# A decoder layer on one core: the expert FFN computed for the chosen tokens only, in 39 static tiles of 128 rows

## The chip, the cores and the metric

The kernel runs on one core of a Trainium2 chip. The metric is the device time of one execution in microseconds. Each comparison is between medians of several runs. The profile is one further execution, and its own time stands beside its span below.

## What is computed

The layer has three parts, each followed by a residual addition and a normalisation without learned scale. The input x has 2048 tokens of width 256.

```
x = norm(x + causal self attention with rotary turns, 16 heads of 16)
x = norm(x + cross attention over one context row per query:
        scores = (x Wq) ctx^T ; idx = argmax ; mem = ctx[idx]
        k, v = mem Wkv ; 16 heads share k and v ; softmax over the 2048 picked rows)
x = norm(x + ffn(x))

ffn: probs = sigmoid(x router^T)            # 8 experts
     topw, sel = top_k(probs, 2); topw /= sum
     h = relu(x W1_e)^2                     # width 256 for experts 0-3, 512 for 4-7
     out = sum over the two chosen experts of topw * (h W2_e)
```

All experts together are 3072 hidden columns wide, which is 24 tiles of 128. Each token needs two experts only.

## The kernel before

The program is a row of blocks. Inside a block each engine has its own list of instructions in a fixed order, and waits on semaphores. Between two blocks all engines meet.

The blocks are the projections with rotary turns, the causal self attention, projection and norm, the choice of a context row for each query, and then one last block with all the rest. The change touches only the last block, apart from small renamings and moved tiles. The last block is entered after a flag is read into a register (`either`). This flag picks the variant for at most 512 distinct context rows.

The last block before the change does two things at once:

- Cross attention in 16 units, for 4 chunks `c` of 512 tokens times 4 groups of heads. A unit has 16 "pieces": TensorE computes 128x512 scores (line 1467) and VectorE reduces each to a row maximum (line 1649). The maxima are turned (1470), negated and written back as extra rows of the operand through a DMA. Then come four steps. In each, TensorE makes four score tiles (1528), ScalarE takes their exponential in two instructions (1617), and TensorE multiplies them with the values (1537). The "sums" item divides (1665, 1671). The pieces of a unit are laid out ahead of the unit's steps by `just_in_time`.
- Everything behind a chunk, as side items laid out by `merge` between the thirds of the attention's steps. There are norm items (turn back 1479, projection 1486, statistics 1686, root 1442 on GpSimd, norm 1696, turn 1492, router logits, gates 1706 to 1725). There are 24 "hid" items per chunk: six matmuls of 512 columns in split fp32r (two parts of each operand, three products, two halves of the contraction, helper `product`, line 95), then relu, square, square on ScalarE (1595, 1599, 1600) and the remainder on VectorE (1729). There are 32 "y" items per chunk, 6 or 12 matmuls of 256 columns each. For each y item VectorE multiplies with the gate and adds to x (1738). Every token goes through every expert, and the gate is zero for six of eight.

Side items share three PSUM banks in turn (`SB`). `merge` gives them out by a budget of columns (`PACE`), so that the FFN of chunk c lies beside the attention of chunk c+1. After the last attention unit the FFN of chunk 3 runs alone. GpSimd splits the weights into two parts early in this block (1431, 1433). It issues no DMA anywhere, all of them go through the SP queue.

## Time and profile before

| | |
|---|---|
| median of 3 runs | 1313.38 us (1313.14 to 1318.69) |
| profiled execution, its own time | 1319.66 us |
| its span, first to last instruction | 1318.0 us |
| PE busy | 1172.4 us (89%) |
| DVE busy | 905.0 us (69%) |
| ACT busy | 674.1 us (51%) |
| POOL busy | 175.6 us (13%) |
| mean granted TensorE clock | 0.934 |

PE is TensorE, PEld its weight loads, DVE VectorE, ACT ScalarE, POOL GpSimd and SP SyncE, which only issues DMAs here. A matmul's busy time contains its latency and overlaps the next one. So the distance between the starts of two matmuls tells more than the length of one.

### The profile page before, as it was taken

The page shows a single profiled execution, that of the slowest core. Times are in us where ns is not written, and L with a number is a line of the kernel's source. Part 1 is how long each engine was busy: PE and PEld are TensorE (multiplying, and loading weights), DVE is VectorE, ACT ScalarE, POOL GpSimd, SP SyncE. Part 2 cuts the span into 40 slices and gives each one's busy share as a digit, 9 for nine tenths or more (in the row PEclk, how much of TensorE's full clock was granted, in tenths as well). Part 3 has the DMA queues.
Part 4 walks back from the last instruction along what each step waited for, and adds up shares of the span by engine and source line. Part 5 has one row for each costly group of instructions (what it writes and reads, how often), then busy time and mean ns, then how long its engine had stood idle before and what let it go on. Part 6 is the DMA issues. An engine that isn't in the chain of part 4 may idle for free. (4 is left out here: it accounts for less than half of the span.)

```text
span 1318.0 us, 18684 instructions
## 1 busy us (share of the span) xinstructions
PE 1172.4 (89%) x6943; PEld 636.2 (48%) x6943; DVE 905.0 (69%) x1799; ACT 674.1 (51%) x951; POOL 175.6 (13%) x167
## 2 busy tenths in 40 slices
PE   6854999999999999974799699899989999999896
PEld 3531233333333333243688423456655665567785
DVE  3564999898888888127499799575657666634543
ACT  1320256666766666842343136456654665575463
POOL 2223111021021100033100265000000000000000
PEclk9885799999999999987799779899989999999999
DMA  6214167920000000030200053000000000000000
GB/s 237 93 49 106 25 75 79 110 28 1 2 1 1 1 1 2 1 134 0 75 26 24 28 163 96 13 13 13 13 13 29 13 13 13 17 1 1 17 1 19
DMA packets 45049, 51.03 MB, mean 39 GB/s; under 512 B 8122, under 2 KB 40506, under 8 KB 44954
## 3 DMA queue, kind: packets, MB, share of 16 engines
q1 hardware_dynamic: 44954, 49.78, 16.6%
q8 instruction: 58, 0.95, 0.3%
q14 instruction: 37, 0.30, 0.1%
HBM read 37.64 MB, written 11.53 MB: 37 GB/s over the span
## 5 line engine op out<-in xcount | busy, mean ns | idle before, releaser
L628 DVE TENSOR_REDUCE self_piece_max<-self_max 128x1 f32<-128x512 f32 (+3 forms) x640 | 349.3, 604 | 52.0 <-PE self_max L530 25.4
L595 ACT ACTIVATE self_probs<-self_scores 128x1024 f32<-128x1024 f32 (+3 forms) x320 | 274.1, 896 | 192.5 <-PE self_scores L549 191.6
L1649 DVE TENSOR_REDUCE cross_piece_max<-banks 128x1 f32<-128x512 f32 x256 | 167.0, 684 | 83.3 <-PE banks L1467 82.8
L530 PE MATMUL self_max<-stack_k,stack_q 96*128 96x512 bf16 (+3 forms) x640 | 209.2, 365 | 12.5 <-DMA stack_k<-kparts 6.4
L1617 ACT ACTIVATE cross_probs<-banks 128x1024 f32<-128x1024 f32 x128 | 128.7, 1018 | 110.0 <-PE banks L1528 109.1
L549 PE MATMUL self_scores<-stack_q,stack_k 98*128 98x512 bf16 (+3 forms) x640 | 170.3, 350 | 4.3 <-DMA stack_q<-self_shift 3.0
L560 PE MATMUL self_out<-self_probs,V 128*17 128x512 f32 (+3 forms) x1280 | 148.3, 535 | 2.6 <-ACT self_probs L595 2.0
L530 PEld LDWEIGHTS self_max<-stack_k,stack_q 96*128 96x128 bf16 x640 | 62.0, 98 | 181.0 <-DVE self_piece_max L628 130.8
L95 PE MATMUL banks<-w_first,hid_first 128*128 128x256 f32 x384 | 118.6, 309 | 7.7 <-DVE hid_rest L1729 4.2
L1595 ACT ACTIVATE o_tok<-banks 128x512 f32<-128x512 f32 x96 | 56.9, 592 | 112.3 <-PE banks L95 111.2
L1729 DVE TENSOR_TENSOR hid_rest<-o_tok,hid_first 128x512 fp32r<-128x512 f32 x96 | 65.5, 687 | 62.1 <-ACT o_tok L1600 61.9
L95 PE MATMUL banks<-w_rest,hid_first 128*128 128x256 f32 x384 | 107.7, 280 | 0.0
L95 PE MATMUL banks<-w_first,hid_rest 128*128 128x256 f32 x384 | 107.6, 280 | 0.0
L1467 PE MATMUL banks<-kx_few,stackx 97*128 97x512 bf16 x256 | 94.0, 408 | 8.4 <-DVE cross_piece_max L1649 4.0
L95 PE MATMUL banks<-x2T_first,w_first 128*128 128x512 f32 x192 | 85.9, 447 | 9.0 <-DVE x2T_rest L1701 7.3
L497 POOL TENSOR_SCALAR_AFFINE_SELECT self_probs<-self_probs 128x512 f32<-128x512 f32 x64 | 40.8, 637 | 397.2 <-ACT self_probs L595 396.9
L1738 DVE SCALAR_TENSOR_TENSOR x_sb<-banks,mix,x_sb 128x256 f32<-128x256 f32 x128 | 60.0, 480 | 41.9 <-PE banks L95 40.7
L95 PEld LDWEIGHTS banks<-w_first,hid_first 128*128 128x128 f32 x384 | 72.8, 190 | 24.1 <-DVE x_sb L1738 9.1
L549 PEld LDWEIGHTS self_scores<-stack_q,stack_k 98*128 98x128 bf16 x640 | 57.0, 98 | 54.0 <-ACT self_probs L595 16.3
L1528 PE MATMUL banks<-stackx,kx_few 99*128 99x512 bf16 x256 | 79.5, 393 | 0.5 <-DMA stackx<-cross_shift 0.5
L95 PE MATMUL banks<-x2T_first,w_rest 128*128 128x512 f32 x192 | 77.4, 403 | 0.0
L95 PE MATMUL banks<-x2T_rest,w_first 128*128 128x512 f32 x192 | 77.3, 402 | 0.0
(219 smaller groups left out, 1704.3 us busy)
## 6 DMA issues: line engine op xcount, KB each, us to landing
stack_q<-qparts SPq DMA_DIRECT2D x96, 64.0 KB, 8.2
stackx<-xparts SPq DMA_DIRECT2D x96, 64.0 KB, 2.3
o_tok<-in_w SPq DMA_DIRECT2D x8, 768.0 KB, 5.6
stack_k<-kparts SPq DMA_DIRECT2D x18, 256.0 KB, 13.1
qparts<-parts SPq DMA_DIRECT2D x8, 384.0 KB, 2.5
kparts<-parts SPq DMA_DIRECT2D x8, 384.0 KB, 2.5
xparts<-xparts_sb SPq DMA_DIRECT2D x8, 384.0 KB, 2.8
xT_sb<-in_xT SPq DMA_DIRECT2D x4, 512.0 KB, 8.1
```

Of the source, the lines that this page charges most:

```text
L95: ins = nc.tensor.matmul(out, lhsT[a], rhs[b], start=first and n == 0, stop=last and n == len(terms) - 1)
L530: mm = nc.tensor.matmul(slot[:, 0:pc["w"]], pc["lhsT"], pc["rhs"], start=True, stop=not pc["diag"])
L549: mm = nc.tensor.matmul(ps[:, j, st["off"]:C], st["keys"](j), st["queries"](j), start=True, stop=True)
L560: mm = nc.tensor.matmul(po[32 * j:32 * j + VW, st["off"]:C], st["values"](j), probs[:, i % 3, j, st["off"]:C], start=st["first"], stop=st[ ...
L595: nc.scalar.activation(probs[:, i % 3, 2 * pair:2 * pair + 2, st["off"]:C], ps[:, 2 * pair:2 * pair + 2, st["off"]:C], ACT.Exp, scale=SCAL ...
L628: nc.vector.tensor_reduce(piece_max[:, u % 2, pc["row"], pc["at"]:pc["at"] + 1], slot[:, 0:pc["w"]], AX.X, ALU.max).then_inc(side_read, 1)
L1467: mm = nc.tensor.matmul(slot[:, 0:pc["w"]], pc["lhsT"], pc["rhs"], start=True, stop=True)
L1528: mm = nc.tensor.matmul(ps[:, j], st["keys"](j), st["queries"](j), start=True, stop=True)
L1617: nc.scalar.activation(probs[:, i % 3, 2 * pair:2 * pair + 2], ps[:, 2 * pair:2 * pair + 2], ACT.Exp, scale=SCALE).then_inc(probs_ready, 1)
L1649: nc.vector.tensor_reduce(piece_max[:, u % 2, pc["row"], pc["at"]:pc["at"] + 1], slot[:, 0:pc["w"]], AX.X, ALU.max).then_inc(side_read, 1)
L1729: nc.vector.tensor_tensor(hid[1][:, h % HR], relu[:, h % 2], hid[0][:, h % HR].bitcast(F32), ALU.subtract).then_inc(hid_ready, 1)
L1738: nc.vector.scalar_tensor_tensor(out=x_sb[:, n], in0=slot[:, 0:D], scalar=mix[:, c % 2, q, e:e + 1], in1=x_sb[:, n], op0=ALU.mult, op1=ALU ...
```

## The change

The last block is split into two.

The first block keeps the cross attention and the norm items. `merge` is replaced by `weave`, a list of items per chunk with fixed distances in thirds of a step. Behind the gates there are new items. "copy" (ScalarE, two copies of the chunk's rows into `xd`). "gate" (VectorE; it writes the weight and the number of the return row beside each row). "rank" (14 tiny matmuls count the tokens before each one in its expert's list, then eight VectorE instructions). "send" (GpSimd, eight indirect DMAs of 128 rows of 258 floats into the expert regions `sent` in device memory). After chunk 3 comes "table", some 20 VectorE instructions on one partition, which make the tables of the 39 tiles: source row, offset in W1, offset in W2. SP then reads eight row numbers into registers and writes eight blocks of padding rows. The weights of W2 are kept four tiles wide for each expert, and VectorE zeroes the unused ones at the block's start.

The second block runs 39 tiles of 128 rows. Of each tile the SP queue loads 128 rows from `sent`, at a row number read into a register, into one of four buffers (`XR`). A buffer is free when the tile that used it has been written back. TensorE turns the rows, computes 512 hidden columns, turns these back, and multiplies with W2. The weight offsets are read into registers on TensorE, twice for each tile. GpSimd writes the 128 result rows with an indirect DMA to `ybuf`. When all 39 tiles are written, both result rows of every token are loaded again, added to x, and x is normalised and stored.

```diff
+TILES = (2 * T + E * (P - 1)) // P          # 39
+ROW = D + 2
+XR = 4
-                def merge(steps, works, first_of, before, thirds):
+                def weave(steps, works, first_of, before, thirds):
+                    todo = [item for c in range(NC) for item in (
+                        ("back", c, 0, 1), ("back", c, 1, 0), ("proj", c, 0, 2), ("proj", c, 1, 0), ("stats", c, 0, 1), ("norm", c, 0, 5),
+                        ("x2t", c, 0, 1), ("x2t", c, 1, 0), ("logit", c, 0, 2), ("ltr", c, 0, 2), ("copy", c, 0, 0), ("gate", c, 0, 1),
+                        ("rank", c, 0, 4), ("send", c, 0, 1))]
...
+                                elif item[0] == "send":
+                                    for q in range(TC):
+                                        for k in range(2):
+                                            nc.gpsimd.indirect_dma_start(
+                                                sent[:], bass.IndirectOffsetOnAxis(place[:, k, q], 0), xd[:, k, q], None).then_inc(s_sent, 16)
+                            pool.wait_ge(probs_used, len(steps))
+                            nc.gpsimd.memset(pads[:, :, 0:D + 1], 0.0).then_inc(pads_ready, 1)
...
+                        sp.wait_ge(pads_ready, 2)
+                        sp.dma_start(sent[E * CAP:].rearrange("(b p) d -> p b d", p=P), pads[:, E:]).then_inc(s_pad, 16)
+                        sp.wait_ge(tab_ready, 1)
+                        for e in range(E):
+                            row = sp.value_load(pad_at[0:1, e:e + 1], min_val=0, max_val=E * CAP - P)
+                            sp.dma_start(sent[bass.ds(row, P)], pads[:, e]).then_inc(s_pad, 16)
...
+                    # SP, second block
+                    for i in range(TILES):
+                        if i >= XR:
+                            sp.wait_ge(s_y[i % XR], 16 * (i // XR))
+                        row = sp.value_load(tab[0:1, 0, i:i + 1], ...)
+                        sp.dma_start(xin[:, i % XR], sent[bass.ds(row, P)]).then_inc(s_xin[i % XR], 16)
+                    # GpSimd
+                    for i in range(TILES):
+                        pool.wait_ge(y_read, i + 1)
+                        nc.gpsimd.indirect_dma_start(ybuf[:], bass.IndirectOffsetOnAxis(xin[:, i % XR, D + 1:ROW].bitcast(U32), 0),
+                                                     ys[:, i % XR], None).then_inc(s_y[i % XR], 16)
+                    # TensorE
+                    for i in range(TILES):
+                        if i + 1 < TILES:
+                            hidden(i + 1)         # value_load, 6 matmuls of 512 columns
+                        if i + 2 < TILES:
+                            turn_in(i + 2)        # waits s_xin, 2 transposes
+                        output(i)                 # value_load, 12 matmuls of 256 columns
+                        if i + 1 < TILES:
+                            turn_back(i + 1)      # 4 transposes
+                    # ScalarE: relu, copy of the turned rows, two squares for each tile
+                    # VectorE: remainder of the rows, scaling of the output, remainder of the squares
+                    # after tile 38: eight loads of 512 KB, two additions (GpSimd, VectorE), statistics, root, norm, 16 stores
```

## Rows read from the trace of the kernel before

**Rows 1.** Windows of the last block: stretch, its length, busy time of each engine, clock, DMA
```profile
751.00:769.60 18.60, 14.14 (x31) 4.08 (x32) 13.03 (x25) 1.28 (x1) 14.36 (x11) 0.50 0.44 142
...
788.30:825.50 37.20, 36.53 (x209) 11.41 (x207) 34.18 (x65) 25.38 (x28) 19.54 (x8) 1.00 0.31 97
...
860.00:1198.00 338.00, 323.20 (x1889) 204.73 (x1888) 209.62 (x468) 197.58 (x292) 4.04 (x4) 0.98 0.05 14
1198.00:1318.00 120.00, 102.83 (x659) 90.33 (x658) 57.59 (x146) 55.50 (x101) 3.02 (x3) 0.98 0.03 10
```

**Rows 2.** Groups from 750.5 us on: busy, mean ns | idle before, releasers
```profile
L1649 DVE TENSOR_REDUCE cross_piece_max<-banks 128x1 f32<-128x512 f32 x256 | 167.0, 684 | 83.3 <-PE banks L1467 82.8
L1617 ACT ACTIVATE cross_probs<-banks 128x1024 f32<-128x1024 f32 x128 | 128.7, 1018 | 110.0 <-PE banks L1528 109.1
L95 PE MATMUL banks<-w_first,hid_first 128*128 128x256 f32 x384 | 118.6, 309 | 7.7 <-DVE hid_rest L1729 4.2 <-DVE x_sb L1738 2.8 <-DVE cross_piece_max L1649 0.4
...
L95 PE MATMUL banks<-x2T_first,w_first 128*128 128x512 f32 x192 | 85.9, 447 | 9.0 <-DVE x2T_rest L1701 7.3 <-DVE x_sb L1738 0.8 <-ACT o_tok L1595 0.2
...
L1729 DVE TENSOR_TENSOR hid_rest<-o_tok,hid_first 128x512 fp32r<-128x512 f32 x96 | 65.5, 687 | 62.1 <-ACT o_tok L1600 61.9
...
L1433 POOL TENSOR_TENSOR w_rest<-o_tok,w_first 128x1536 fp32r<-128x1536 f32 x8 | 27.5, 3442 | 0.6
...
L1607 ACT COPY cross_acc<-banks 128x512 f32<-128x512 f32 x16 | 9.3, 579 | 6.4 <-PE banks L1537 6.4
```

**Rows 3.** Chain that ended last: start, us, what
```profile
1228.80 4.42 PE banks L95 x18
...
1292.19 7.26 PE banks L95 x54
```

**Rows 4.** Writers of banks, 769 to 826 us: durations, first and last start
```profile
L1665 DVE RECIPROCAL cross_inverse<-banks x4: 246/248/248, 788.3 to 825.5; 128x16 f32<-128x16 f32 x4
```

**Rows 5.** Timeline of DVE, 828 to 845 us: start, us, what, idle before
```profile
828.74 0.69 DVE L1649 TENSOR_REDUCE cross_piece_max<-banks 128x1 f32<-128x512 f32 x1 [1.96 <-PE banks L1467]
...
831.51 0.69 DVE L1677 TENSOR_TENSOR x_sb<-banks,x_sb 128x512 f32<-128x512 f32 x1 [0.64 <-PE banks L1486]
833.24 0.69 DVE L1677 TENSOR_TENSOR x_sb<-banks,x_sb 128x512 f32<-128x512 f32 x1 [1.03 <-PE banks L1486]
...
844.00 1.29 DVE L1701 TENSOR_TENSOR x2T_rest<-banks,x2T_first 128x512 fp32r<-128x512 f32 x2 [0.83 <-ACT x2T_first L1581]
```

**Rows 6.** Timeline of chunk 3 behind its attention
```profile
1198.99 1.04 PE L1479 MATMUL banks<-ident,o_tok 128*128 128x128 f32 x8
...
1202.15 3.69 PE L1486 MATMUL banks<-xwc_sb,o_tok 128*128 128x256 f32 x16 [0.63 <-ACT o_tok L1577]
...
1207.69 1.40 DVE L1686 BATCH_NORM_STATS2 norm_stats<-x_sb 128x6 f32<-128x256 f32 x4
...
1209.85 1.01 POOL L1442 TENSOR_TENSOR norm_rstd<-norm_rstd,minus_half 128x4 f32<-128x4 f32 x1 [68.70 <-DVE norm_rstd L1691]
```

**Rows 7.** Timeline of the gates of chunk 0, first and last of 22 instructions
```profile
859.00 0.17 DVE L1706 TENSOR_SCALAR gate<-gate 128x32 f32<-128x32 f32 x1
...
861.91 0.19 DVE L1723 TENSOR_TENSOR hot<-hot,top 128x32 f32<-128x32 f32 x1
```

**Rows 8.** Timeline at the entry of the last block
```profile
749.88 0.59 ACT L1046 CAST kx_few<-pp 99x512 bf16<-99x512 f32 x1 [2.06 <-PE pp L1008]
...
751.47 1.28 ACT L1617 ACT_TABLE_LOAD   x1 [1.01 <-PEq L910]
```

**Rows 9.** DMA issues: what, count, KB each, median us from issue to landing
```profile
stackx<-xparts SPq DMA_DIRECT2D x96, 64.0 KB, 2.3
...
out<-x_sb SPq DMA_DIRECT2D x16, 128.0 KB, 1.8
...
x_sb<-in_x SPq DMA_DIRECT2D x1, 1536.0 KB, 8.8
```

**Rows 10.** SP's issues of the tile stackx: ns min/median/max, first and last start
```profile
L1376 SPq DMA_DIRECT2D stackx<-xparts x96: 303/426/1888, 750.9 to 1094.3; - x96
```

More of the change, by code:

```diff
@@ L44 @@
 SX = 4
-HR = 6
-PACE = 0.9
 LOW = -3.0e38
@@ L139, in decoder_layer @@
         tri_b = sb(top, "tri_b", [P, P], BF16)
+        ones_b = sb(top, "ones_b", [P, P], BF16)
+        below_b = sb(top, "below_b", [P, P], BF16)
         consts_in = sem("consts_in")
@@ L515, in program @@
                             loaded, reads, freed = [0], [0], []
-                            nc.tensor.matmul(po[:], zeros[:, 0:P], zeros[:], start=True, stop=True)
+                            for n in range(C // P):
+                                nc.tensor.matmul(po[:, n * P:(n + 1) * P], zeros[:], zeros[:], start=True, stop=True)
                             def side_item(item):
@@ L1197, in plan @@
-            def plan(keys, vals, n):
-                steps, works = [], []
-                width = C if n == FEW else n // 4
-                for c in range(NC):
-                    for g in range(NG):
-                        u = c * NG + g
-                        here = stackx[:, u % SX]
-                        pieces = [dict(w=width, lhsT=here[0:KS + 1, j, q * P:(q + 1) * P],
-                                       rhs=keys[0:KS + 1, a * width:(a + 1) * width], row=j * GH + q, at=a)
-                                  for j in range(GH) for q in range(C // P) for a in range(n // width)]
-                        works.append(dict(pieces=pieces, shift_to=[
-                            here[KS + 1 + b:KS + 2 + b].rearrange("o h (n t) -> o (h n) t", t=P) for b in range(2)]))
-                        for t in range(n // P):
-                            steps.append(dict(unit=u, diag=0, first=t == 0, last=t == n // P - 1,
-                                              keys=lambda j, t=t: keys[0:KS + 3, t * P:(t + 1) * P],
-                                              queries=lambda j, u=u: stackx[0:KS + 3, u % SX, j, :],
-                                              values=lambda j, t=t: vals(t)))
-                return steps, works
@@ L1217, in columns @@
-            def columns(item):
-                kind = item[0]
-                if kind in ("hid", "logit"):
-                    return 3 * KD * C
-                if kind == "y":
-                    return 3 * (WIDTHS[item[2]] // P) * D
-                if kind == "proj":
-                    return 4 * 2 * KD * D
-                return 4 * C if kind in ("back", "x2t") else 0
-            def just_in_time(steps, works):
-                per, length = len(works[0]["pieces"]), len(steps) // len(works)
-                maxima = [("piece", u, k) for u in range(len(works)) for k in range(per)]
-                given = per + per // 3
-                before = maxima[0:per] + [("turn", 0)] + maxima[per:given]
-                thirds = [[[], [], []] for _ in range(len(steps) + 3)]
-                late = []
-                for i in range(len(steps)):
-                    want = min(len(maxima), per + -(-per * (i + 3) // length))
-                    new = maxima[given:want]
-                    given = max(given, want)
-                    for k in range(3):
-                        late = [(n - 1, item) for n, item in late]
-                        thirds[i][k] += [item for n, item in late if n == 0]
-                        late = [(n, item) for n, item in late if n]
-                        mine = new[(k * len(new) + 2) // 3:((k + 1) * len(new) + 2) // 3]
-                        thirds[i][k] += mine
-                        late += [(2, ("turn", item[1])) for item in mine if item[2] == per - 1]
-                assert not late and given == len(maxima)
-                for i, step in enumerate(steps):
-                    if step["last"]:
-                        thirds[i + 2][0].append(("sums", step["unit"]))
-                return steps, works, {u: u * length for u in range(len(works))}, before, thirds
@@ L1355, in decoder_layer @@
[L1355 to L1368 removed]
+            stage = ExitStack()
@@ new lines, in decoder_layer @@
+            xin = sb(tail, "xin", [P, XR, ROW])
+            xT = [sb(tail, f"xT_{n}", [P, 2, KD, P], F32R) for n in ("first", "rest")]
+            act_of = sb(tail, "act_of", [P, 2, C])
+            hT = [sb(tail, f"hT_{n}", [P, 2, 4, P], F32R) for n in ("first", "rest")]
+            square = sb(tail, "square", [P, 2, C])
+            ys = sb(tail, "ys", [P, XR, D])
+            yb = sb(tail, "yb", [P, 2, NT, D])
+            px = psum(tail, "px", [P, 2, C])
+            ph = psum(tail, "ph", [P, 2, C])
@@ L1434, in _ @@
-                    pool.wait_ge(w_split, len(pieces_w) + 1)
-                    def program(steps, works, first_of, before, slots, at, read_at, copied_at, norm_at, stat_at):
-                        order = [it for step in slots for slot in step for it in slot if it[0] in ("stats", "fstats")]
-                        for k, (_, c) in enumerate(order):
-                            mine = rstd[:, TC * c:TC * (c + 1)]
-                            pool.wait_ge(s_ones2, SX + 1)
-                            pool.wait_ge(var_ready, k + 1)
-                            nc.gpsimd.tensor_tensor(mine, mine, minus_half[:], ALU.pow).then_inc(rstd_ready, 1)
@@ L1628, in _ @@
+                    turned_in(1)
+                    positive(0)
+                    squares(0)
+                    for i in range(TILES):
+                        if i + 1 < TILES:
+                            positive(i + 1)
+                        if i + 2 < TILES:
+                            turned_in(i + 2)
+                        if i + 1 < TILES:
+                            squares(i + 1)
                 @block.vector
                 def _(dve):
-                    chained = Count(sem("cross_dve_chain"))
@@ new lines, in _ @@
+                    turned_in(0)
+                    turned_in(1)
+                    rests(0)
+                    for i in range(TILES):
+                        if i + 2 < TILES:
+                            turned_in(i + 2)
+                        dve.wait_ge(y_ready, i + 1)
+                        if i >= XR:
+                            dve.wait_ge(s_y[i % XR], 16 * (i // XR))
+                        nc.vector.tensor_scalar(ys[:, i % XR], py[:, i % 2, 0:D], xin[:, i % XR, D:D + 1], None, ALU.mult).then_inc(y_read, 1)
+                        if i + 1 < TILES:
+                            rests(i + 1)
```

1171 lines of the change are left out of this document (668 added, 503 removed).

## The prediction

> **What bounds the kernel now.** I read the windows of the last block first [rows 1], since the change leaves the 751 us ahead of it alone. The block is 567 us long. In its first attention chunk, which has no FFN beside it, DVE is busy 34.2 of 37.2 us: attention alone is bound by the row maxima. From 860 us on PE is busy 323 of 338 us and DVE only 210: with the FFN beside it TensorE is the limit. The last 120 us are the FFN of chunk 3 by itself. Next the groups [rows 2]: the FFN is 576 matmuls of 512 columns (three groups of 192) and 1152 of 256 columns (three of 384). Their busy times overlap, so I take the distance between starts from the chain [rows 3]: 4.42 us for 18 matmuls of 512 columns is 0.245 us each, 7.26 us for 54 of 256 is 0.134 us. The FFN so costs 576 x 0.245 + 1152 x 0.134 = 141 + 154 = 295 us of TensorE. It falls to 234 x 0.245 + 468 x 0.134 = 57 + 63 = 120 us, plus turns. So 175 us leave TensorE. But they leave a block in which they lay beside DVE-bound attention, and what comes back is serial.
>
> **First block, attention with routing (from 751 us).** The attention of chunk 0 stays as it is. Its divisions are at 788.3 and 825.5 us, three units apart [rows 4]: 12.4 us for a unit of four steps, 3.1 us a step. The same pace holds for the following units, as there is no FFN to slow them, and DVE is what they wait for. From step 17 (825.5) to step 58, the last with pieces, are 41 steps: 127 us, to 952. To this come DVE's new and kept items for chunks 0 to 2, which sit on the binding engine and so count in full. For each chunk these are the projection's two additions 1.4; statistics 2.0 (1.4 for four [rows 6], aggregates 0.6); norm 1.4; two remainders 1.3 [rows 5]; gates 4.2 (22 instructions took 3.1 us from 859.0 to 862.1 [rows 7], now they are 25 with more of them waiting for the one before); rank about ten instructions of this size, 2.0. Sum 12.3. In that order DVE also waits: 1.96, 0.64, 1.03 and 0.83 us for PE and ACT in chunk 0 [rows 5], 4.5 us, and I take 5, between nothing and 8. So 3 x 17.3 = 52 us, to 1004. The remaining seven steps have no maxima and go at ACT's pace, 2 x 1.02 us [rows 2], with a last copy, turn and division: 15 us. The attention ends at 1019 us. In the kernel before, that point was 1198. ACT has room (25.4 of 37.2 us in three units [rows 1]). TensorE's records fill 36.5 of the 37.2 us, but they overlap, and by starts it has some too. GpSimd splits two more weight pieces, each two thirds of (1.5 + 3.4) us, in time for the first turn back by my estimate. Zeroing W2 on DVE (eight instructions of 128x512, 0.35 to 0.69 us each) lies in the 5 us in which DVE waits for the first operand; without this cover it is 5 us.
>
> **Behind chunk 3, all serial.** Turn back 1.0 and ACT 0.6, projection 3.7 (PE, 16 matmuls [rows 6]), addition 0.7, statistics 2.0, root 1.0, norm 1.4, turn, copy and remainder 2.5, logits 2.1, gate turn 0.7, gates 4.2, rank 1.2 on PE and 2.0 on DVE: with about 0.1 us for each handover 24 us, to 1043. Then GpSimd issues eight scatters of 128 rows. The trace has no indirect DMA. The nearest row below is SP's issue, 0.43 us [rows 10], the nearest above GpSimd's longest instruction, 3.44 us [rows 2]. I take 1.5 us, nearer to the issue since this is no elementwise work. So 12 us. GpSimd's list has the memset of the padding (3855 elements a partition, at its 1 us for a thousand, 4 us) behind them, and SP waits for it: 1059. The table on DVE (20 instructions, 6 us) is covered by this. SP issues one store, then eight times a register load and an issue. The entry of the old block bounds a register load with barrier, compare and branch at 1.0 us (750.47 to 751.47 [rows 8]) and so the load alone between 0 and 1; I take 0.5. Nine issues and eight loads are 8 us, landing 2, meeting of the engines 1: the second block starts at 1070 us (1061 to 1086).
>
> The Trainium skill (DMA: Bandwidth & Descriptors, Latency and other measured facts) puts the floor of a register load from memory at about 600 ns. By it the eight loads would be 0.8 us longer and the sum 0.8 us later.
>
> **The tiles.** Two loops compete.
> (a) TensorE in its own order: 6 x 0.245 + 12 x 0.134 + 6 turns x 0.13 (eight in 1.04 us [rows 6]) = 1.47 + 1.61 + 0.78 = 3.86 us. Two register loads come on top, each between 0 (queued matmuls cover it) and 1.0 us; I take 0.3, which makes 4.5. ACT has 0.37 + 3 x 0.58 = 2.1 us and DVE 0.4 + 0.4 + 0.69 = 1.5 us for a tile [rows 2]; both have room.
> (b) The return of a buffer. The turn of tile i+2 waits for the write-back of tile i-2. From the end of output(i-2): DVE's scaling 0.4, scatter issue 1.5, landing of 128 KB in device memory 1.8 [rows 9], SP's register load and issue 0.9, landing of the load 2.0 (between 1.8 and 2.3 [rows 9]), five handovers 0.5: 7.1 us. TensorE needs two periods less output(i-1) and one turn (1.9 us) to get there, so 2 P - 1.9 >= 7.1, P >= 4.5. With the scatter at 0.43 us P is 3.95, at 3.44 us it is 5.45.
> Both come to 4.5, and two loops of the same length on in-order engines lose a little: P = 4.7 us. The first tile needs 8.5 us from the start to the end of its output, 38 periods are 178.6, the last write-back 4.3: 191.4, to 1261.5 us.
>
> **The end.** Eight loads of 512 KB: 2 MB in all for the first two chunks, 4 MB by 18.6 us, at the rate of the 1.5 MB load behind the 0.5 MB one (2 MB in 9.3 us [rows 9]). Then for chunks 2 and 3, which no transfer covers any more: GpSimd's addition of 1024 elements 2.3 (3.44 for 1536), DVE's addition 1.3 and statistics 2.1, twice, norm 1.4 three times, handovers, last store 1.8: 15.9 us. Together 34.5, to 1296 us of span. The old end had 8 us from its last output to the last instruction.
>
> **Sum.** 751 + 268 + 51 + 191.4 + 34.5 = 1296 us of span against 1318.0, 22 us less. The profiled execution took 1319.66 us, 1.66 around its span, so its like is 1297.6. The median of the runs is 6.3 us below the profiled one; taken from the median, 1313.4 - 22 = 1291 us. Of the 175 us that leave TensorE 22 remain, since routing, padding, the fill of the tiles and the return are now behind one another.
>
> **Rivals.**
> (1) Cheaper DMAs: the scatter costs as little as SP's issue. P falls to about 4.0, bound by TensorE's 3.86 with register loads hidden: 38 x 0.7 = 27 us less, and 8 x 1.07 = 9 us less behind chunk 3. Time 1291 - 36 = 1255. For it: matmuls queue far ahead in this trace, with hardly a gap in L95's groups [rows 2]. Against: GpSimd computes each of 128 addresses, SP does not.
> (2) Slower than before: the scatter itself is dear, up to 3.44 us on GpSimd. It is paid 8 times behind chunk 3 (+15.5 us) and stands in loop (b), P = 5.45 (+28.5 us): 1335 us. Each further microsecond of scatter costs 8 + 19 = 27 us, so this decides from 2.3 us on, where the 22 us are gone. For it: small GpSimd work is slow here, four elements a partition take 1.01 us [rows 6]. Against: nothing but the guess of its kind.
> (3) The clock. In the stretch at the block's entry, where TensorE waited 0.5 us between single matmuls, 0.50 of full speed was granted (the 1.2 GHz level), and 1.00 (2.4 GHz) where it was dense [rows 1]. In the tile loop it works 3.9 of 4.7 us. If a sixth of the time went at the lower level, loop (a) is 5.1 us: +15 us, 1306.
> (4) GpSimd and DVE in each other's way. Rows first: GpSimd's eight subtractions took 3.44 us on the mean beside DVE's reductions from PSUM [rows 2], and no row shows what an instruction of DVE with SBUF operands does to them. In the tiles DVE's remainder of the squares has two operands in SBUF, 0.69 us. If it holds back the scatter each time, loop (b) is 0.69 longer, P + 0.35, +13 us: 1304. The Trainium skill (SBUF — State Buffer, the "DVE blocks DMA" trap) says that DVE instructions holding the shared port keep GpSimd from writing its descriptors; that rule speaks for this rival, and no row of this trace shows an indirect DMA.
>
> **Chances.** Forecast 0.40, (1) 0.17, (2) 0.25, (3) 0.08, (4) 0.10. The forecast's own range is 1274 to 1310. Measurements of this kernel tell about 0.5% (6.6 us) from no change: faster is below 1306.8, slower above 1320. Of the forecast 0.36 lies below that and 0.04 within; (1) is all faster, (3) and (4) fall half below and half within, (2) is slower but for 0.02. With a margin for unlisted stalls, which only lengthen: faster 0.56, same 0.15, slower 0.29. The range is 1250 to 1348: from a little under (1) to a little over (2).
>
> **What would show it.** The attention's last division near 1019 us with 12.4 us units; if later, routing stalls DVE or TensorE more than 5 us a chunk. GpSimd's scatter at 1.5 us; the second block's first load at 1070. Starts of the tiles' outputs 4.7 us apart, and TensorE's longest wait in a tile: if it is for the landed rows, loop (b) holds; if for nothing or for registers, loop (a). The last 35 us without matmuls. The prediction is wrong if the scatter takes over 2.3 us, if the tiles' period leaves 4.0 to 5.4, or if the serial piece behind chunk 3 is longer than 65 us.

## The result, and the profile of the changed kernel

The changed kernel takes 1309.2 us in the median of 12 runs (1301.62 to 1312.03); the kernel before took 1316.42 (12 runs, 1311.28 to 1321.62) beside it. The ratio is 0.9933, interval [0.9908, 0.9958]: about 7 us less, where 22 were forecast. The profiled execution took 1306.89 us, with a span of 1305.1 and a granted clock of 0.898. The same kernel run later (e10, two runs), on the chip that had e5 to e9, took 1300.76 and 1295.11 us, ratio 0.9869 [0.9833, 0.9905] to the kernel before beside it.

The page of the changed kernel: busy times, then groups (busy, mean ns, idle before), then DMA issues.

```profile
PE 1054.4 (81%) x6214; PEld 522.4 (40%) x6214; DVE 876.0 (67%) x1759; ACT 599.2 (46%) x827; POOL 261.0 (20%) x249
...
L1619 DVE TENSOR_REDUCE cross_piece_max<-banks 128x1 f32<-128x512 f32 x256 | 164.0, 683 | 30.4 <-PE banks L1441 25.5
...
L1786 POOL DMA_INDIRECT ybuf<-ys,xin x39 | 37.5, 960 | 160.4 <-DVE ys L1916 160.4
...
L1409 POOL DMA_INDIRECT sent<-xd,expert_place x32 | 31.3, 979 | 100.1 <-DVE chosen_b L1707 87.1
...
xin<-sent SPq DMA_DIRECT2D x39, 129.0 KB, 2.1
```

DVE's idle time before a row maximum fell from 83.3 to 30.4 us [rows 2]: the attention now goes at DVE's pace, as forecast. The scatter, which no row of before showed, takes 0.96 us of GpSimd. The windows show which limit replaces TensorE (columns as in [rows 1]): the serial piece behind the attention, then the tiles.

```profile
1028.40:1083.77 55.37, 10.48 (x57) 6.91 (x57) 16.20 (x71) 4.89 (x8) 12.47 (x11) 0.64 0.17 57
1100.00:1260.00 160.00, 136.61 (x836) 114.73 (x835) 55.55 (x104) 69.78 (x140) 33.59 (x35) 0.97 0.19 59
```

For 55 us no engine is busy a third of the time. In the tiles TensorE records 137 of 160 us, and this view of the waits between 1100 and 1268 us (total us, times, longest us) says what it waits for:

```profile
POOL ybuf L1786 <- DVE ys L1916: 134.3, 38, 6.0
...
PEld px L1812 <- DMA xin<-sent: 22.9, 18, 3.1
PE px L1812 <- DMA xin<-sent: 15.2, 17, 2.6
PEld py L1840 <- issue: 13.8, 21, 1.0
```

The same stretch as the chain of waits tells it, one turn of a buffer (start, us, what):

```profile
1095.90 0.50 DVE ys L1916
1096.39 0.27 issue
1096.66 2.40 DMA ybuf<-ys,xin
1099.07 0.27 SPq L1769
1099.37 0.15 SPq L1769
...
1099.79 2.11 DMA xin<-sent
1101.95 0.44 PE px L1812 x2
1102.38 0.41 issue
1102.80 1.24 PE py L1840 x8
1104.03 0.50 PE py L1843 x4
1104.55 0.50 DVE ys L1916
```

From a tile's scaling at 1095.90 to the turn of the tile that takes its buffer at 1101.95 are 6.05 us, and to the scaling of the tile two further on 8.65 us. That is two periods: loop (b), as forecast. At first the outputs follow each other at 3.48 and 5.1 us in turn. Later the distances lie between 3.5 and 5.4 us, with four longer ones (6.0, 6.2, 7.4, 6.9) and the last two at 3.3 and 3.1; the mean is 4.49. A wait for rows stands in about every second tile (18 for 38). The 0.41 us of "issue" behind the turn is the place of a register load. TensorE's first product of the output starts 0.85 us after the turn here, and 0.84 us in e2, where the turn takes 0.69 rather than 0.44 us. That the load sets this distance is argued, no run leaves it out.

The span in the prediction's terms, for the two profiled executions of the changed kernel ("again" is the later one) and the combined version further down. The first division is the first L1635 RECIPROCAL, the last its 16th; the second block starts with the first xin load; an output is a tile's L1916.

| term, us | forecast | changed | again | combined |
|---|---|---|---|---|
| start to first division | 788.3 | 792.4 | 791.5 | 786.5 |
| first to last division | 230.7 | 236.0 | 230.7 | 229.9 |
| last division to second block | 51 | 55.3 | 55.5 | 43.2 |
| second block to first output | 8.5 | 12.1 | 14.2 | 13.7 |
| 38 periods | 178.6 | 170.8 | 168.6 | 132.1 |
| last output to the end | 38.8 | 38.4 | 38.5 | 34.7 |
| span | 1296 | 1305.1 | 1299.0 | 1240.0 |

### The profile page after: what moved, and what is told of

Same layout as the page of the kernel before. It is cut to its first block and busy times, and to the rows that moved or that the text cites. A ratio compares the mean times of both kernels' runs of the same rounds, so it can differ in the third digit from the quotient of the medians.

```text
span 1305.1 us, 17932 instructions
## 1 busy us (share of the span) xinstructions
PE 1054.4 (81%) x6214; PEld 522.4 (40%) x6214; DVE 876.0 (67%) x1759; ACT 599.2 (46%) x827; POOL 261.0 (20%) x249
## 5 line engine op out<-in xcount | busy, mean ns | idle before, releaser
L538 PE MATMUL self_max<-stack_k,stack_q 96*128 96x512 bf16 (+3 forms) x640 | 209.4, 365 | 12.6 <-DMA stack_k<-kparts 6.4
L1619 DVE TENSOR_REDUCE cross_piece_max<-banks 128x1 f32<-128x512 f32 x256 | 164.0, 683 | 30.4 <-PE banks L1441 25.5
L1441 PE MATMUL banks<-kx_few,stackx 97*128 97x512 bf16 x256 | 95.3, 412 | 21.3 <-DVE cross_piece_max L1619 12.3
L1513 PE MATMUL banks<-cross_probs,vx_few 128*17 128x512 f32 x512 | 71.8, 635 | 0.4 <-ACT cross_probs L1583 0.4
L1441 PEld LDWEIGHTS banks<-kx_few,stackx 97*128 97x128 bf16 x256 | 25.4, 100 | 112.6 <-DVE cross_piece_max L1619 61.2
L1786 POOL DMA_INDIRECT ybuf<-ys,xin x39 | 37.5, 960 | 160.4 <-DVE ys L1916 160.4
L1899 DVE TENSOR_TENSOR xT_rest<-px,xT_first 128x256 fp32r<-128x256 f32 x39 | 16.6, 425 | 62.9 <-ACT xT_first L1865 62.8
L540 PE MATMUL self_max<-tri_b,ident_b 128*128 128x128 bf16 x256 | 58.5, 231 | 0.0
L1904 DVE TENSOR_TENSOR hT_rest<-square,hT_first 128x512 fp32r<-128x512 f32 x39 | 27.0, 692 | 46.9 <-ACT square L1879 46.9
L1878 ACT ACTIVATE hT_first<-pt 128x512 fp32r<-128x512 f32 x39 | 23.3, 598 | 70.0 <-PE pt L1829 70.0
L1812 PE MATMUL px<-ident,xin 128*128 128x128 f32 x78 | 16.2, 293 | 47.9 <-DMA xin<-sent 47.9
L1409 POOL DMA_INDIRECT sent<-xd,expert_place x32 | 31.3, 979 | 100.1 <-DVE chosen_b L1707 87.1
L98 PE MATMUL pp<-ctx_first,qp_first 128*128 128x512 f32 (+1 forms) x128 | 46.7, 365 | 3.2 <-DVE qp_rest L1065 2.0
```

The lines of the kernel that those rows point to most:

```text
L98: ins = nc.tensor.matmul(out, lhsT[a], rhs[b], start=first and n == 0, stop=last and n == len(terms) - 1)
L538: mm = nc.tensor.matmul(slot[:, 0:pc["w"]], pc["lhsT"], pc["rhs"], start=True, stop=not pc["diag"])
L540: mm = nc.tensor.matmul(slot[:, pc["w"] - P:pc["w"]], ident_b[:], tri_b[:], start=False, stop=True)
L1441: mm = nc.tensor.matmul(slot[:, 0:pc["w"]], pc["lhsT"], pc["rhs"], start=True, stop=True)
L1513: mm = nc.tensor.matmul(po[32 * j:32 * j + VW], st["values"](j), probs[:, i % 3, j], start=st["first"], stop=st["last"], tile_position=(0, ...
L1619: nc.vector.tensor_reduce(piece_max[:, u % 2, pc["row"], pc["at"]:pc["at"] + 1], slot[:, 0:pc["w"]], AX.X, ALU.max).then_inc(side_read, 1)
```

## Experiments

The theory behind them was this: the tiles go at the return of their buffers; zeroing and the serial piece take what is missing; the chunks' work costs more than its instructions since TensorE's turns and projections are spaced wrongly. The rivals are told in the expectations. All except the fourth edit the changed kernel; e10 is that kernel without an edit.

**e1: a ring of eight buffers.**

```diff
-XR = 4
+XR = 8
```

(The semaphores of the eight loads are ones that the block before has done with; that part of the edit is not shown.)

> Eight row buffers and result buffers instead of four (XR = 8), nothing else. Theory (the return of a buffer sets the period): with four buffers two tiles share one return of about 9 us, so outputs come 3.5 and 5.2 us apart, 4.49 on the mean. With eight, the return has six periods and binds no more; TensorE's own order is left, which the short periods of the changed kernel show as 3.5 us. 38 x (4.49 - 3.55) = 36 us less: tiles' outputs 3.5 to 3.6 us apart, time about 1273 us. Rival (register loads and TensorE's issue set the period, the waits for landed rows are only where that slack shows): period stays between 4.3 and 4.5, time within 5 us of the changed kernel, 1304 to 1314.

Measured: 1273.11 us (1272.01 to 1277.37), ratio 0.967 [0.9654, 0.9687]. Outputs are 3.49 us apart, and no wait for xin is left; the window, the waits of the tiles, and the outputs' line:

```profile
1120.00:1220.00 100.00, 100.00 (x691) 91.00 (x690) 46.01 (x87) 55.45 (x115) 26.92 (x28) 1.00 0.24 75
```

```profile
POOL ybuf L1787 <- DVE ys L1917: 91.0, 36, 2.9
ACT hT_first L1879 <- PE pt L1830: 44.4, 36, 1.3
```

```profile
L1917 DVE TENSOR_SCALAR ys<-py,xin x39: 482/484/486, 1104.1 to 1236.2; 128x256 f32<-128x256 f32 x39
```

38 periods last 132.1 us rather than 170.8. TensorE's own order is 3.48 us a tile. The forecast had 3.86 for its work alone, so the matmuls are a little cheaper than taken, and the 0.6 us for register loads in loop (a) do not show where matmuls are queued. This execution's attention was the longest of all (last division 1034.2), so 39 us in the tiles show as 30 in its span.

**e2: a ring of three**, `XR = 3`.

> Three buffers instead of four. Theory (return of a buffer): the turn of tile i+2 now waits for the write-back of tile i-1, one period less 1.7 us of TensorE after its output. The return itself takes 7.1 us (two mean periods of 4.49 less 1.9), so the period is 7.1 + 1.7 = 8.8 us, 38 x 4.3 = 164 us more: about 1470 us. Rival (TensorE's own order): the return has slack today, so the period is at most 5.5 us and the time at most 1350.

Measured: 1492.57 us, a single execution. The period is 9.75 us for most tiles (38 last 358.6 us), and TensorE waits for the rows in every tile (waits, then the window):

```profile
PEld px L1812 <- DMA xin<-sent: 118.3, 30, 4.6
```

```profile
1120.00:1440.00 320.00, 196.25 (x790) 162.25 (x789) 52.42 (x99) 67.47 (x131) 31.73 (x33) 0.74 0.09 28
```

With three buffers one period is a whole return and TensorE's part behind it. In one turn of the chain the return from scaling to turn takes 5.97 us (1151.56 to 1157.53), much as with four buffers. TensorE's part behind it takes 3.81 us rather than 2.60. The mean granted clock is 0.74 of full speed, so part of the stretch is at the lower level; TensorE is busy 196 of its 320 us. At 2.60 the period would be 8.6 us, at 3.81 it is 9.8. The expectation had 8.8 with a longer return and no loss of clock; it came out 23 us short, 0.6 us a tile. So rival (3) is real, but only with waits longer than those that four buffers leave: with four the clock is 0.97. Both experiments say the same: what four buffers cost is the return.

**e3: zeroing W2 on ScalarE** rather than on DVE.

```diff
...
-                                nc.vector.tensor_copy(w[:, e, 2:4].rearrange("p t (a d) -> p (t a) d", d=P),
-                                                      zeros[:].rearrange("p (a d) -> p a d", a=1).to_broadcast([P, 4, P]))
+                                nc.scalar.copy(w[:, e, 2:4].rearrange("p t (a d) -> p (t a) d", d=P),
+                                               zeros[:].rearrange("p (a d) -> p a d", a=1).to_broadcast([P, 4, P]))
...
```

> The eight instructions that zero the unused part of W2 run on ScalarE instead of VectorE; nothing else. Theory (VectorE's four copies of 2.09 us were held by GpSimd's memsets of the operand's ones rows, which run in the same 8 us): VectorE is free when the first scores are there, the first row maximum ends 4 to 5 us earlier, and all that follows is DVE-bound, so the time falls by 4 to 5 us: 1304 to 1305. Rival (the late start comes from the loads of the first operand, or ACT's copies now delay the first exponentials): within 1.5 us of the changed kernel.

Measured: 1300.58 us (1297.76 to 1306.91), ratio 0.9892 [0.987, 0.9914]. The timelines of the changed kernel and of this one at the block's entry:

```profile
749.78 8.12 DVE L1603 CAST w_first<-zeros 128x512 fp32r<-128x512 f32 x4 [1.94 <-PEq L916]
757.83 1.45 DVE L1603 CAST w_rest<-zeros 128x512 fp32r<-128x512 f32 x4
...
760.14 2.49 DVE L1619 TENSOR_REDUCE cross_piece_max<-banks 128x1 f32<-128x512 f32 x4 [0.73 <-DVE cross_piece_max L1605]
...
749.74 7.88 POOL L1380 MEMSET stackx<- 1x2048 bf16 x4 [115.43 <-POOLq L916]
```

```profile
750.38 2.17 ACT L1542 CAST w_first<-zeros 128x512 fp32r<-128x512 f32 x4 [0.45 <-PEq L916]
...
750.36 7.37 POOL L1380 MEMSET stackx<- 1x2048 bf16 x4 [116.40 <-POOLq L916]
...
755.55 4.87 DVE L1620 TENSOR_REDUCE cross_piece_max<-banks 128x1 f32<-128x512 f32 x8 [4.93 <-PE banks L1441]
```

Four casts of DVE take 8.12 us beside GpSimd's memsets, one cast to a memset, and the next four take 1.45: 2.03 us each against 0.36. On ScalarE the same casts beside the same memsets take 0.54 us each. The first row maximum begins 4.6 us sooner, and DVE waits 4.93 us for its operand: the cover was there, but the zeroing was twice its length. That the memsets make the casts slow is read from the two timelines, where each of the four casts begins up to 0.15 us behind a memset and ends 0.28 us behind it; no run leaves the memsets out. The rest of the median's 8.6 us is not shown to be this edit's. In the profiled execution it lies in the tiles, whose 38 periods took 166.1 us rather than 170.8, and this term moves without an edit too (168.6 us in e10).

The Trainium skill (SBUF — State Buffer, Who interferes with whom) says of the port pair that DVE and GpSimd share that, against a DVE instruction in a mode with two ports, whoever issues first holds it for the whole instruction. The durations agree, with 2.03 us for 0.36 us of work; the profile does not show the ports. The prediction weighed this only for the scatters in the tiles.

**e4: the dense kernel of before without its FFN.**

```diff
-                hidden = list(tiles)
+                hidden = []
-                values = [(c, e, q) for c in range(NC) for e in range(E) for q in range(TC)]
+                values = []
```

> The kernel before without its FFN: the hid, rest and y items are left out (the output is the normalised attention part alone); router, gates and both norms stay. Theory (attention and routing are bound by VectorE at 12.4 us a unit and 17 us of chunk work, so the dense FFN filled only TensorE's slack and cost nearly its whole length): the last division comes near 1018 us, the chain behind it about 30 us, end at 1050 us; the dense FFN so costs 265 of its 295 us, and the sparse one, 255 us with routing, fill, return and padding, is only 10 us shorter. Rival (the interleaving hides a good half of the dense FFN): the time is 1150 us or more.

Measured: 1056.45 us (two runs), ratio 0.8026 [0.8006, 0.8046]. The output of this kernel is the normalised attention part alone. Its divisions lie between 787.8 and 1024.1 us (1018 expected). That is 236.3 us, against 236.0 in the changed kernel, which starts them 4.6 us later. DVE and TensorE between them:

```profile
830.00:1010.00 180.00, 154.98 (x817) 54.23 (x815) 149.02 (x373) 94.04 (x107) 6.07 (x6) 0.93 0.10 30
```

The dense FFN costs 1316.4 - 1056.5 = 260 us of the time, for 295 us of TensorE: only 35 lay in the attention's shadow. The sparse one with its routing costs 1309.2 - 1056.5 = 253, for 39 x 3.48 = 136 us of TensorE. So 117 us of it are something else than TensorE's work in the tiles: routing, what became serial, and waits.

**e5: the padding not cleared**, its row numbers written ahead of chunk 3's scatters rather than behind them.

```diff
                                 elif item[0] == "send":
+                                    if c == NC - 1:
+                                        pool.wait_ge(probs_used, len(steps))
+                                        nc.gpsimd.tensor_copy(pads[:, :, D + 1:ROW].bitcast(U32),
+                                                              places_sb[:, 2 * NT:].rearrange("p (b o) -> p b o", o=1)).then_inc(pads_ready, 1)
...
-                            nc.gpsimd.memset(pads[:, :, 0:D + 1], 0.0).then_inc(pads_ready, 1)
...
```

> The padding is no longer cleared (its rows go to places nobody reads), and its row numbers are written ahead of chunk 3's eight scatters instead of behind them. Theory (behind chunk 3 the padding is queued behind the scatters on GpSimd, and SP's eight loads and stores behind the padding): SP starts when the table is ready, 1059.7 instead of 1070.5 on the clock of the changed kernel, needs some 11 us and 2 us of landing, and the scatters' own end at 1069 is covered; the second block starts 10 us earlier, time 1299. Rival (the meeting of the engines waits for the landing of the scatters or for something else): at most 3 us, 1306.

Measured: 1286.2 us (1281.88 to 1293.47), ratio 0.9775 [0.9744, 0.9806]. GpSimd, and SP's padding stores, in the changed kernel:

```profile
1054.33 1.04 POOL L1409 DMA_INDIRECT sent<-xd,expert_place  x1 [15.54 <-DVE chosen_b L1707]
...
1058.34 0.96 POOL L1409 DMA_INDIRECT sent<-xd,expert_place  x1 [0.31 <-issue]
1062.15 0.97 POOL L1409 DMA_INDIRECT sent<-xd,expert_place  x1 [2.85 <-issue]
...
1066.90 3.34 POOL L1413 MEMSET cross_probs<- 128x3855 f32 x1
...
1070.54 0.41 SPq L1365 DMA_DIRECT2D sent<-cross_probs  x1
1071.82 8.88 SPq L1369 DMA_DIRECT2D sent<-cross_probs  x8
1083.77 1.53 SPq L1770 DMA_DIRECT2D xin<-sent  x2
```

and SP here:

```profile
1038.02 0.41 SPq L1365 DMA_DIRECT2D sent<-cross_probs  x1
1059.14 8.68 SPq L1369 DMA_DIRECT2D sent<-cross_probs  x8
1070.76 4.10 SPq L1769 DMA_DIRECT2D xin<-sent  x4
```

The stores now lie beside the scatters. From the last division to the second block it is 45.0 us, against 55.1 to 55.8 in six executions of kernels that leave this piece alone: 10.3 us, as expected. The edit does two things, and what each gives by itself is not separated. The 23 us between the medians are not this edit's gain: beside the changed kernel on the same chip (e10, 1297.9 us, two runs) it is 11.7.

**e6: the second turns back and their successors one or two thirds later.**

```diff
-                        ("back", c, 0, 1), ("back", c, 1, 0), ("proj", c, 0, 2), ("proj", c, 1, 0), ...
-                        ("x2t", c, 0, 1), ("x2t", c, 1, 0),
+                        ("back", c, 0, 1), ("back", c, 1, 1), ("proj", c, 0, 2), ("proj", c, 1, 2), ...
+                        ("x2t", c, 0, 1), ("x2t", c, 1, 1),
```

> The second turn back, the second half of the projection and the second turn of a chunk go one or two thirds of a step behind the first instead of right behind it; no work changes. In the changed kernel a chunk costs 17.6 to 20.2 us over four plain units, of which VectorE's own instructions are about 13. Theory (the rest is VectorE waiting for TensorE's and ScalarE's part of an item that stands directly ahead of it, 4.5 us a chunk in the trace): with pieces between, some 2 to 3 us a chunk are won back, 6 to 9 us in all, 1300 to 1303 us. Rival (the wait is set by the three shared PSUM banks and only moves): within 2 us of the changed kernel, 1307 to 1311.

Measured: 1300.08 us (1294.32 to 1304.62), ratio 0.9876 [0.9845, 0.9907]. Against 1309.2 us it looked like a hit, and it was not one: the unedited kernel on the same chip takes 1297.9 us (e10, two runs), and from its first to its last division 230.7 us, where this one has 231.3.

**e7: combined**: ring of eight, zeroing on ScalarE, padding not cleared, one semaphore for each chunk of returned rows.

```diff
-                                         ).then_inc(s_yb[c // 2], 16)
+                                         ).then_inc(s_yb[c], 16)
```

> Eight buffers, W2 zeroed on ScalarE, padding ahead of the scatters, and one semaphore for each of the four chunks of returned rows instead of one for two. If the places are independent: 1309 - 36 (measured for eight buffers) - 8.6 (measured for the zeroing, of which the trace explains 4.3) - 10 - 4 for the tail (VectorE starts after 1 MB of rows instead of 2 MB; the last rows land as before) = 1251 to 1255 us. Rival (the return's slack with eight buffers already contains part of the others): 1258 or more.

Measured: 1242.25 us (1241.45 to 1247.52), ratio 0.9453 [0.9428, 0.9479]. Here is the tiles' window, and the end, where GpSimd's first addition has to wait for 1 MB and no longer for two:

```profile
1080.00:1200.00 120.00, 120.00 (x826) 109.08 (x825) 54.90 (x103) 66.83 (x138) 32.95 (x35) 1.00 0.23 72
```

```profile
1214.16 2.33 POOL L1793 TENSOR_TENSOR x_sb<-x_sb,yb 128x1024 f32<-128x1024 f32 x1 [7.13 <-DMA yb<-ybuf]
```

Against "again", by the table: tiles -36.5, serial piece -12.3, start -5.0, end -3.8, attention -0.8 and first tile -0.5, sum -59 us of span. The effects add up, and three of them are where their single experiment had them (tiles -38.7 in e1, start -4.6 in e3, serial piece -10.3 in e5). The semaphore for each chunk had no experiment of its own. The kernel beats both others, and is 9 us below the expectation, which was summed from 1309.2 us and not from this chip's 1297.9.

**e8: combined, half of the padding stores on ScalarE's queue.**

```diff
-                        for e in range(E):
+                        for e in range(E // 2):
...
+                        for e in range(E // 2, E):
+                            row = act.value_load(pad_at[0:1, e:e + 1], min_val=0, max_val=E * CAP - P)
+                            act.dma_start(sent[bass.ds(row, P)], pads[:, e]).then_inc(s_pad, 16)
```

> As the combined kernel, with four of the eight register loads and padding stores behind chunk 3 issued from ScalarE's queue. Theory (SP's eight at 1.22 us each end after the scatters' landing): SP and ACT need 5 us each, the end is then set by the scatters, 2 to 4 us less than the combined kernel. Rival (the scatters set it already): no difference.

Measured: 1244.97 us (1242.84 to 1247.01), ratio 0.9459 [0.9436, 0.9483]. From the last division to the second block it is 43.0 us, 43.2 without this edit, so the 2 to 4 us of the theory did not come. The stores did go out earlier: the last one was issued 37.1 us behind the last division rather than 39.8. But ScalarE's four took 3.3 to 4.5 us to land, where SP's eight of the combined version take 2.1 to 3.0, and the last store landed at 41.6 rather than 41.9 us. The last scatter landed at 41.8 us here. In the combined version SP's wait for the stores ends with their last landing, and its wait for the scatters behind it costs nothing. So stores and scatters end together, and a second queue moves only the issues. That the transfers slow each other is argued. Behind the landings come the blocks' meeting and a register load, 1.2 us.

**e9: combined, with e6's spacing.**

> The combined version (ring of eight, zeroing on ScalarE, padding not cleared, one semaphore for each chunk of returned rows) with the later second turns back, projections and transposes of the spacing experiment. If the chunks' work stalls DVE by its spacing whatever lies around it, the last division comes 3 to 5 us earlier than in the combined version (1016.4 us there) and the time falls from 1242.3 to about 1238. Rival: the -9 us of the spacing experiment's medians were mostly from the tiles' period, which the ring of eight has already taken: last division within 2 us of 1016.4, time 1241 to 1243.

Measured: 1242.97 us (1240.53 to 1243.6), ratio 0.9443 [0.9423, 0.9463]. From the first to the last division it is 231.4 us, against 229.9 without the spacing. The rival's 1241 to 1243 us is met, though the last division is 3.3 us later than in the combined version (1019.7 and 1016.4), and the theory of the spacing falls.

**e10: the changed kernel once more.**

> The changed kernel itself a second time, no edit. If the tiles' period is settled by chance in each execution (the return of a buffer against TensorE's order), the 38 periods last a time other than 170.8 us by more than 2 us, while the first division (792.4 us) and the distance from the last division (1028.4) to the second block's first load (1083.8, 55.3 us) stay within 1 us. Rival: the schedule repeats exactly, 4.49 us a tile, and what the medians of the single edits gained beyond their traces comes from elsewhere.

Measured: 1297.93 us, ratio 0.9869 [0.9833, 0.9905], the two runs told at the top. Its divisions, and its outputs:

```profile
L1635 DVE RECIPROCAL cross_inverse<-banks x16: 245/247/258, 791.5 to 1022.2; 128x16 f32<-128x16 f32 x16
...
L1916 DVE TENSOR_SCALAR ys<-py,xin x39: 482/484/485, 1091.9 to 1260.5; 128x256 f32<-128x256 f32 x39
```

The tiles took 168.6 us rather than 170.8, a difference of just over 2 us, as expected, and the serial piece 55.5 rather than 55.3. What was not expected: the attention took 5.3 us less. By chips, from the first to the last division: 240.6, 236.4 and 236.4 us in e1 to e3, which ran on one chip; 229.9 to 231.4 in the six executions of e5 to e10, on another; 236.0 in the profiled execution of the changed kernel, whose chip is not on record. The kernel before shows no such step (medians 1315.64, 1316.42 and 1315.48 us in three jobs on these two chips). What in a chip makes it stays open. But the traces show where a good part of it is lost. In all four long executions DVE pauses for 2.3 to 2.5 us about 18 us ahead of the last division, and that unit takes 13.3 to 13.5 us, against 9.7 to 11.7 in the six short ones. In e1 DVE and ScalarE pause together once more, and restart together:

```profile
878.31 2.48 DVE L1619 TENSOR_REDUCE cross_piece_max<-banks 128x1 f32<-128x512 f32 x4 [3.45 <-remote]
878.35 1.94 ACT L1583 ACTIVATE cross_probs<-banks 128x1024 f32<-128x1024 f32 x2 [4.35 <-remote]
```

"remote" stands where the profile ties the end of a wait to no instruction and no transfer of the program. That unit took 18.1 us instead of 12.4. No such pause of DVE stands in the attention of the six short executions. The granted clock fell behind the pause: in e1 it was 1.00 from 872 to 878 us and 0.50 from 881 to 884. So the lower clock of e1's stretch from 868 to 943 us is at least in part a consequence (e1, then e7):

```profile
868.00:943.00 75.00, 65.78 (x341) 22.93 (x340) 56.96 (x137) 40.01 (x46) 11.53 (x13) 0.89 0.13 42
```

```profile
868.00:943.00 75.00, 68.28 (x392) 24.09 (x392) 64.05 (x152) 45.08 (x52) 10.22 (x11) 0.98 0.15 46
```

## Why the prediction was wrong, point by point

The direction and most of the mechanisms were right; the gain was a third of what was forecast. By its own steps:

- **"The attention stays as it is ... 3 x 17.3 us"**: right as a mechanism, and right in size in "again": 230.7 us between the divisions, and 16.7 and 17.4 us for the first two chunks, so it is no sum of errors that cancel. It is 5.3 us short in the profiled execution (17.6 and 19.7 us for the two). The forecast came from one execution and had no width for it; from one chip to another this term differs by that much.
- **"Zeroing W2 on DVE lies in the 5 us in which DVE waits"**: failed, 4.1 us at the first division. Eight instructions at 0.35 to 0.69 us fit into 5 us; at 2.03 us for the first four they took 9.5. The named price without cover, 5 us, was right.
- **The serial piece, 51 us**: 4.3 short. To rank 25 us rather than 24. The eight scatters took 12.6 from first start to the memset, 12 forecast: each is cheaper (0.96 and 0.30 to the next, not 1.5) but one pause of 2.85 us stands among them. Memset 3.34, not 4. From the memset at 1066.90 to the second block at 1083.77 it is 16.9 us, put at 15: SP's nine issues and eight register loads took 10.2 us, not 8. The handover to GpSimd, 0.8 us, is the rest.
- **The first tile, 8.5 us**: 3.6 to 5.7 short. Two things were left out. TensorE came out of the serial piece at 0.50 of full speed, its 1.2 GHz level, and its first six products of hidden rows took 2.94 us where the next six took 1.66. In "again" and in the combined version the next six were at the lower level too (0.63 us each, as the first), which is the 2 us between 12.1 and 14.2. And in TensorE's order the second tile's products and turn stand ahead of the first tile's output. The windows:

```profile
1083.77:1091.20 7.43, 4.11 (x10) 2.40 (x10) 0.85 (x2) 0.80 (x3) 0.00 (x0) 0.50 0.27 73
1091.20:1096.00 4.80, 4.10 (x27) 3.55 (x28) 1.22 (x3) 2.49 (x5) 0.00 (x0) 1.00 0.01 2
```

- **The tiles, P = 4.7**: 4.49 and 4.44. Loop (b) held by itself, as e1 and e2 show from both sides. Its return was 6.05 us, not 7.1 (scatter 1.5 taken), TensorE's part 2.6, not 1.9; (6.05 + 2.6) / 2 = 4.33, and some landings take longer (3.06 and 4.38 us for two scatters in the chain, where 2.4 is the median). That the sum of (b) came out at 4.5 is partly luck: the return was put 1.05 us too long and TensorE's part 0.7 us too short. Loop (a) was put at 4.5 and is 3.48: so the two were not of one length, and there was nothing to add for their meeting.
- **The end**, 38.8 against 38.4: the size came out by luck. The last of the eight loads landed 13.4 us after the first was issued, not 18.6. From there to the end it was 21.8 us, not 15.9: the additions, statistics and norms of GpSimd and DVE stand behind one another, and the chain waits for no load after 1277.93. The two engines also held each other up: DVE's first addition took 3.28 us beside GpSimd's second, the others 1.22, and GpSimd's last took 3.45 us beside one of DVE, 2.33 alone.

```profile
1280.37 3.28 DVE L1924 TENSOR_TENSOR x_sb<-x_sb,yb 128x1024 f32<-128x1024 f32 x1 [13.21 <-POOL x_sb L1792]
...
1285.61 1.23 DVE L1924 TENSOR_TENSOR x_sb<-x_sb,yb 128x1024 f32<-128x1024 f32 x1
...
1291.26 3.45 POOL L1792 TENSOR_TENSOR x_sb<-x_sb,yb 128x1024 f32<-128x1024 f32 x1
```

The terms so add up to 9 us of span more than forecast (4.1 + 5.3 + 4.3 + 3.6 - 7.8 - 0.4), and "again" to 3. **The step that failed by its own reason is the zeroing at nothing**: its cover was half its length, and it cost 4.1 us. It does not carry the miss alone. Beside it two terms were mis-sized, the serial piece (51 for 55.3) and the fill of the tiles (8.5 for 12.1). The three are 12 us, of which the cheaper tiles gave 8 back; the attention's 5.3 are in the one execution and not in the other. The other 5.6 us of the miss are no term: the profiled execution of before lies 3.2 us above the median of its 12 runs, the changed one's 2.3 below.

The rivals: (1) was half right. The scatter is cheap, yet P did not fall to TensorE's, because landing twice, not issuing, makes the return. (2) fell with 0.96 us. (3) is absent at four buffers (0.97), there at three (0.74), and present where it wasn't looked for, in the first tile. (4) did not hold a scatter back in the tiles (0.954 to 0.989 us over 39). A conflict of the two engines came elsewhere: at the attention's start GpSimd held DVE, and at the end each held the other once.

Behind this: in a ring of four a buffer comes back and its tile is worked on in 8.65 us at best, in which two tiles go through with 7.0 us of TensorE's work. This, zeroing, padding and one semaphore gave away 56 of the 74 us that lie between the kernel before and the combined version (1316.4, 1297.9 and 1242.3 us).

The Trainium skill (DMA: Bandwidth & Descriptors, Anatomy of one DMA — SWDGE (gpsimd) path) fits such a transfer with 2.0 us plus bytes by 436 thousand per us: 2.3 us for 128 KB, an estimate. The trace agrees, with 2.4 us as the median from the scatter's start to its landing. GpSimd's 0.96 us lie within these 2.4, while the prediction laid 1.5 us of issue ahead of the 1.8 us of a plain store: 3.3 in all.

## What to carry to other kernels

A ring through device memory has two landings in its return: count buffers by return divided by period, and add where a wait shows at every second item. (Here five should do, as an estimate: the 8.65 us would then have three periods of 3.48 us, 10.4 us. Only three, four and eight were run.) When work moves out of a shadow, sum what becomes serial first; it was 55 us here, of which 10 went by writing the padding's row numbers earlier and not clearing its rows. For a stage that waits at its entry, look at what the neighbour on the shared port does in that time. And before an edit of a few microseconds is believed, run the unedited kernel on the same chip, and compare the term that the edit touches.

## What the runs showed of the hardware

- An indirect scatter of 128 rows of 1 KB: 0.96 us on GpSimd, 1.27 us from one start to the next, 2.4 us from its start to landing. In all ten executions of kernels with scatters GpSimd pauses after the fourth of chunk 3's eight, for 2.67 to 3.01 us, and after the sixth of chunk 1's, for 2.12 to 2.82 us. That is behind the 14th and the 28th of the 32; the series of chunks 0 and 2 have no pause. The cause stays open.
- Four fp32 casts of DVE from SBUF to SBUF beside GpSimd memsets: 2.03 us each, one to a memset; 0.36 behind them.
- Additions of 128x1024 with both operands in SBUF, on DVE and GpSimd at once: DVE 3.28 us rather than 1.22 where GpSimd was ahead, GpSimd 3.45 rather than 2.33 where the two started together.
- A register load with the issue that needs it: 1.1 us on SP in a row of eight (8.88 us). On TensorE, between queued matmuls, nothing that can be seen (3.48 us a tile in e1). Behind a wait, 0.41 us of idle time stand in its place.
- TensorE at 0.50 of full speed after a stretch of 55 us in which it was busy for 10.5, and at 1.00 from the second tile's products on in one execution. In three others (e10, e1, e7) these products were still at the lower level.
